# Three matrix products that nobody reads, after each middle group of the next tile, in a graph network's gather stage

## The reference

```python
msg  = concat(h[src], h[dst]) @ Mw.T + Mb          # one message per arc
s1, s2 = segment_sum(msg, dst), segment_sum(msg * msg, dst)
mx, mn = segment_max(msg, dst), segment_min(msg, dst)
mean = s1 / deg; var = relu(s2 / deg - mean * mean); std = sqrt(var + 1e-30)
agg  = concat(mx, mn, std, var)                     # 4 x 128 per node
u    = concat(h, agg, agg * a(deg), agg * b(deg)) @ Uw.T + Ub
u    = batchnorm(u)                                 # over the nodes
h    = elu(layernorm(leaky_relu(u @ mix.T + mb) + h))
```

## Time and profile before

| | |
|---|---|
| three runs | 2149.43 us median, 2140.32 to 2154.02 |
| profiled execution, span from first to last instruction | 2141.7 us |
| granted clock of TensorE, mean over the span | 0.661 of full speed |
| busy: PE, PEld, DVE, ACT, POOL | 682.6, 402.8, 1096.6, 455.6, 1235.7 us |
| indirect gathers of stage A | 1161 |

### The profile page before, as it was taken

The page is one execution under the profiler, slowest core; times in us unless marked ns, Lnnn a source line. Parts: engine busy times, 40 slices in busy tenths (PEclk is TensorE's granted clock), DMA queues, the critical chain, the costliest instruction groups (busy, mean ns, idle before and its releaser), DMA issues. The chain is left out here.

```text
span 2141.7 us, 10446 instructions
## 1 busy us (share of the span) xinstructions
PE 682.6 (32%) x2156; PEld 402.8 (19%) x2156; DVE 1096.6 (51%) x2178; ACT 455.6 (21%) x1024; POOL 1235.7 (58%) x1358
## 2 busy tenths in 40 slices
PE   5611233132322470323132232362113322233265
PEld 5311121011111230112111111131101211112122
DVE  8600755464644843445464463572525664466464
ACT  0103321122111154111111111136101221112125
POOL 7673666676666127745675675406756666576504
PEclk9975666565655685566565666686556666656677
DMA  4363333333333033323332232204323333333200
GB/s 59 105 167 113 93 103 103 91 99 92 92 91 91 18 112 113 111 66 99 96 101 76 88 103 75 65 27 145 106 84 101 93 88 93 88 103 96 76 0 30
DMA packets 97107, 190.18 MB, mean 89 GB/s; under 512 B 30792, under 2 KB 56984, under 8 KB 97040
## 3 DMA queue, kind: packets, MB, share of 16 engines
q0 software_dynamic: 59968, 160.78, 26.6%
q1 hardware_dynamic: 37077, 28.77, 4.9%
HBM read 168.75 MB, written 17.75 MB: 87 GB/s over the span
## 5 line engine op out<-in xcount | busy, mean ns | idle before, releaser
L742 POOL DMA_INDIRECT G<-p_by_rank,index x774 | 734.8, 949 | 560.2 <-issue 227.8
L742 POOL DMA_INDIRECT G<-p_by_node,index x387 | 367.4, 949 | 225.0 <-issue 120.3
L921 PE MATMUL ps<-wide_ident,agg 128*128 128x128 f32 x288 | 80.3, 434 | 1209.3 <-issue 701.2
L1470 DVE TENSOR_TENSOR ps<-ps,G 128x1024 f32<-128x1024 f32 (+3 forms) x222 | 250.3, 1127 | 191.2 <-issue 78.4
L921 PEld LDWEIGHTS ps<-wide_ident,agg 128*128 128x128 f32 x288 | 51.5, 217 | 1239.5 <-issue 721.9
L936 PE MATMUL ps<-w_u_sb,aggT 128*128 128x384 f32 x576 | 284.3, 654 | 0.0
L1714 DVE SCALAR_TENSOR_TENSOR var<-tot,rdeg,msq 128x128 f32<-128x128 f32 x75 | 26.1, 348 | 426.4 <-ACT msq L1109 407.8
L936 PEld LDWEIGHTS ps<-w_u_sb,aggT 128*128 128x128 f32 x576 | 162.6, 282 | 144.7 <-issue 119.1
L1135 ACT ACTIVATE u_sb<-ps 128x128 f32<-128x128 f32 x75 | 20.7, 277 | 721.1 <-remote 509.0
L1472 DVE TENSOR_TENSOR ps<-ps,G 128x512 f32<-128x512 f32 (+3 forms) x222 | 141.6, 638 | 0.0
L1471 DVE TENSOR_TENSOR ps<-ps,G 128x512 f32<-128x512 f32 (+3 forms) x222 | 141.5, 637 | 0.0
(11 more groups left out here) (280 smaller groups left out, 1328.3 us busy)
## 6 DMA issues: line engine op xcount, KB each, us to landing
G<-p_by_rank,index POOLq DMA_INDIRECT x774
p_by_rank<-base SPq DMA_DIRECT2D x18, 512.0 KB
G<-p_by_node,index POOLq DMA_INDIRECT x387
p_by_node<-G SPq DMA_DIRECT2D x6, 514.0 KB
w_u_sb<-in_w_u SPq DMA_DIRECT2D x3, 768.0 KB
x_r<-rows_by_rank SPq DMA_DIRECT2D x1, 1600.0 KB
G<-shared_rows SPq DMA_DIRECT2D x12, 53.0 KB
windows<-src_pad SPq DMA_DIRECT2D x1, 624.8 KB, 14.1
```

Of the source, the lines that this page charges most:

```text
L742: g.indirect_dma_start(G[:, n % R, j, 0:w], None, table, bass.IndirectOffsetOnAxis(ap=named, axis=0))\
L921: ins = nc.tensor.transpose(ps[:, 2, i * D:(i + 1) * D], agg[:, t % 2, i * D:(i + 1) * D], ident[:, :])
L1470: TT(run[:, 0:nk, :], run[:, 0:nk, :], G[:, n % R, 0:nk, 0:2 * D], ALU.add)
```

## The change

After the work of tile t on PE, for t below FAR = 21, `unread_products` is called. It waits until ACT has copied the transposed aggregates of tile t out of bank 2, and then, for each middle group of tile t+1 (all but its first and its last), until DVE has taken that group in, and issues three products of 128x384 into bank 2. Nobody reads them; the next transposes overwrite them. All other instructions stay as they were.

```diff
@@ -882,6 +882,14 @@
                 for _ in range(count):
                     mm(ps[:, 3, :], ident[:, :], hT[:, 0:4 * D], start=True, stop=True)
 
+            def unread_products(l, t):
+
+                pe.wait_ge(agg_copied.sem, agg_copied.at(l, t + 1))
+                for n in range(tile_groups[t + 1][1], tile_groups[t + 1][-1]):
+                    pe.wait_ge(dve_used.sem, dve_used.at(l, n + 1))
+                    for i in range(3):
+                        mm(ps[:, 2, 0:3 * D], ident[:, :], w_u_sb[:, i, :], start=True, stop=True)
+
             def update_last(l):
                 t, z = T - 1, ps[:, 4, 0:3 * D]
                 parts = (ps[:, 2, 0:2 * D], ps[:, 0, 0:2 * D])
@@ -978,6 +986,8 @@
                         idle_products(2)
                     if t == 1:
                         lend(l)
+                    if t < FAR:
+                        unread_products(l, t)
```

## The result

The changed kernel takes 2209.34 us (median of 4 runs, 2201.14 to 2216.69), the kernel before 2149.91 us beside it: ratio 1.0288, 95% interval 1.0263 to 1.0314. The sign was right, the size was not: some 60 us came instead of 390, and 2209 lies near the lower end of a range that had been drawn around 2540. In the table of the experiments medians are of all executions, while ratios and intervals leave out two of the six of e10, the only ones that fell into a slower state.

A forecast was written before the change was run, and what follows sets the result against it. PE's completions, late while gathers flow, were taken to hold up ACT, DVE and POOL (276 us). Added cost of 145 us per layer, 435 in all, took 2141.7 to about 2577; less some 40, forecast 2540 us, range 2130 to 2950.

The forecast's parts named there:

- Step 1: PE before the unread products: the wait for ACT's copy is open after 0.6 us and delays nothing.
- Step 2: Unread products at full pace: six passes of 654 ns, 3.9 us per middle group, hidden beside POOL's 5.0 us.
- Step 3: Unread products at 1.15 us per instruction: 13.8 us per middle group, 1739 us as upper bound.
- Step 4: Cycle of two four-group tiles in stage A: 58 us, 29 each against 22.5, so +6.5 us per tile.
- the reserve of 41: About 41 PE instructions complete on time beside gathers before the slow price; pauses give them back, DMA silence at once.
- C's burst: First tile's PE work in the cycle, begun with whole reserve: passes in 7 us; its 24 unread instructions then take 28.
- D's transposes: Second tile of the cycle: crawl from 35 to about 44 us; POOL falls silent at 38.
- E's burst: Third tile of the cycle: begins at 58 us, like the first, closing a pair of tiles.
- Step 5: Sum over stage A's tiles: 85, 48 and 12 us, 145 per layer, 435 us for three layers.
- The first: Rival: lateness comes from TensorE cooling between tiles, unread products fill the gaps; faster, about 1900 us; chance 0.12.
- The second: Rival: added instructions ride in PE's waiting time, 27.6 us per tile hidden; about 2150 us; chance 0.07.
- The third: Rival: silence never comes or gives nothing, 1.15 us per instruction through stage A; about 3300 us; chance 0.05.

The follow-up runs named there:

- e10: Kernel before, with POOL waiting for the product of tile t - 3 ahead of the second group of tile t: 2122.01 us, ratio 0.9853.
- probe3: Separate measuring kernel, transposes beside gathers after rests, in bursts of several sizes: 48 instructions took 8.3 us, 96 took 52, 192 took 156.
- e3: Changed kernel with six unread products per middle group instead of three, 3024 added instructions: 2255.62 us, ratio 1.0485 to the kernel before.
- e5: Kernel before with one of the four products of aggT in each update, 864 instructions fewer: 2079.50 us, ratio 0.9681.
- probe: Separate kernel timing TensorE's completions alone and beside other traffic: a burst of 128 instructions took 10 us alone, 97 us beside gathers.

## Why the prediction was wrong

**Right: the mechanism and its place.** TensorE's completions are late beside gathers, by instructions and not by columns, and POOL's stops for DVE are where the time is lost. The experiments on count, columns and neighbours all went that way.

**Step 1, the wait for `agg_copied`, half right.** It is open in tiles that are on time. In late tiles it holds PE back, 478.5 us in 20 times, which I had not seen. It seems to do no harm, and even good: the unread products of a late tile are issued behind the release, next to a silence (542.11 in the cycle above), where they pass. No run leaves this wait out.

**Step 2 right:** six passes at 594 ns are 3.6 us beside POOL's 5.0.

**Step 3 right in kind:** 1.40 us in the long run where I had 1.15 from the earlier trace rows, bursts whose quick beginning was averaged in.

**Step 4 failed: how many instructions pass before a tile is late.** It took the reserve of 41 as spent by C's burst and the beginning of its unread products, so that 28 us of slow completions followed and every second tile was late, 58 us for two. What layer 1 shows in its place:

- The reserve. Between POOL's restart after a stop of over 6.5 us and the first transposes or product read more than 2 us late, PE issued 48, 41, 50, 39, 50 and 37 instructions in the kernel before, and 90, 92, 87, 87, 64, 88 and 92 in the changed one. The 41 fit the kernel before; with unread products twice as many pass, so most of the 1512 never paid the slow price, and in four cycles of seven three tiles fit between two stops.
- The cycle. The three cycles of two tiles took 53.6, 57.3 and 52.7 us, near the 58 of the forecast; the four of three tiles 20.4 to 25.9 us per tile. The mean over 18 tiles is 24.1, not 29.
- Inside the cycle of 1135.23 POOL is silent at 48 (forecast 38), D's transposes are read at 48, just before the silence (35 to 44), and E's burst comes at 57 (58). In layer 0, from C's burst at 508.53, POOL is silent at 27.9, stopped by ACT's ranks, which the cycle had left out; D's transposes are released together with the rest at 32.9, not one by one; and E's burst comes at 41.1, since DVE had E's sums complete when it stopped (528.87) and needed only the variance.

Why more of them pass than the 40 to 50 of probe3 is open. The reserve may not be a number of instructions at all: counted in time, the first late result was due 15 to 26 us after the restart in the kernel before and 13 to 24 in the changed one, nearly the same, and in probe3 a second burst of 30, 25 us behind the first gather, was late at once. Against time alone stand the transposes at 855, quick after 71 us of gathers, since 783.97. No run separates the two.

From tile 3 to tile 21, by the times at which ACT reads the transposes, the tile became longer by 0.7 us in layer 0, 1.6 in layer 1 and 1.3 in layer 2, where 6.5 was forecast for tiles with two middle groups; times 18 that is 66 us, the measured loss.

**Step 5 followed from it:** 435 us where 66 came. Two bounds of the range don't follow from their own words either: half of 435 above 2142 is 2360 only without the 40 us that the forecast takes off, and two thirds of two thirds of 435 are 193, which gives 2335 and not 2270. The error behind the arithmetic is one of kind. I priced a queue by its length, but its consumer is stopped by a ring of 14 buffers, and each stop both bounds the loss (some 15 us) and empties the queue. With twice the added instructions the loss is 107 us, where I had put 600 by that pricing.

**The rivals.** The first (a cooling TensorE) falls: the clock rose from 0.661 to 0.709, and to 0.739 in e3, while the time rose; in e5 it fell to 0.587 and the kernel was faster. The rule of the Trainium skill ("TensorE: Matmul & The Clock Gate", section "Why this matters for your kernels") that bursts should not be parted by idle gaps, so that the clock stays up, describes the clock correctly here and predicts the time with the wrong sign. The second (no change, the pauses give the reserve back faster than I think) had the right correction to my numbers, and the truth lies nearer to it than to my forecast: I gave it 0.07, since I had only rows 4 and 5 for the effect of a silence. The third falls with e3. The page "SBUF — State Buffer" of the Trainium skill (section "Who interferes with whom") says that DMA never contends with a compute engine; for plain transfers the probe agrees (10 us with and without), for POOL's gathers a burst takes 97 us instead of 10. Whether that is contention for SBUF at all, no run here shows; that bytes and rows don't matter speaks against it.

**What would have shown it:** ACT's L1145 should have risen and fell, since the lateness is now met at L1139; DVE's L1724 rose, as said (468), and PE's L929 waits less for ACT (121 us, before 501); POOL's waits for DVE rose to 261 us, not to 500.

## What to carry to other kernels

Where TensorE's results are needed beside a stream of gathers, count its instructions, passes and weight loads, against the time between natural stops of the stream, and look at when its semaphore is read, not at when its instructions are recorded. Where a lateness ends in a full ring that silences its own cause, the loss is stops times the price of a stop; work out that cycle from the trace before pricing what is added. Here a stop of the gathers that waits for a late product gave 1.0 to 1.5% over the kernel before when it began at tile 4, and cost 0.6 to 1.2% when it began at tile 7.

## What the runs showed of the hardware that I had not expected

- POOL's indirect gathers make TensorE's semaphore increments late; plain transfers of more bytes do not, nor do POOL's memsets (128 instructions: 97, 10 and 9 us). Gathers of 16 rows or of 256-byte rows do it as much as 128 rows of 1 KB (107 and 92.5 us).
- The long-run price is 1.40 us per TensorE instruction, increments standing on a grid of 0.70 us: 5.60 us for four instructions, 8.4 for six, 11.2 for eight, the same for transposes, for products of 384 columns and for bf16 ones. In probe3 the first 40 to 50 after a rest are nearly free; in the changed kernel's layer 1 64 to 92 pass after a stop of POOL.
- The instructions are recorded at full pace meanwhile, dozens ahead of their completions; in probe3 the first gap between them shows after five bursts and a half, at 1282.5, when some 170 are recorded and 78 complete; from there on they are recorded at 1.40 us each too. A product that is recorded is not a product that can be read.
- After POOL's last gather the slow price goes on, mostly for 4 to 8 us in the kernels and for 27 us in probe and probe3; then what is outstanding is released within a few microseconds. A pause of 5.8 us just ahead of a burst let it pass; the same pause in the middle of one did not (89.7 us).
- By what path the gathers do this, and what makes the quick beginning of a burst longer or shorter, stays open.
- One candidate for the path is the recording. Every timed execution here lists a span and a granted clock, so none shows TensorE unrecorded. The Trainium skill ("NOTIFIC — the notification-queue block", section "7.1 Overflow: three behaviours, one of which stalls the engine") says that the block that writes records holds back its producers when its own buffers are full, rather than lose a record. A price per instruction whatever its size, after dozens that are free, would fit that; no run here tells it from a cause outside the recording.
